# Gated recurrent attention block: the rest term carried inside the step products, Wi's product in whole float32, and a new loop order

## The reference

```python
def step(carry, xs):                 # over the 128 times
    r = decay * r + kt * vt          # kt = vt = ctx
    retained = qt * r                # qt = layernorm(x)
    inp = retained @ Wi.T + bi
    gate = sigmoid(inp @ Wg.T + bg)
    blended = gate * state + (1.0 - gate) * inp
    state = tanh(blended @ A.T + inp @ Bm.T)
    out = state @ Wo.T + bo
x = x + tanh(g_xattn) * out
h = relu(layernorm(x) @ ternary(W1).T + b1)
x = x + tanh(g_ffn) * (h @ ternary(W2) + b2)
```

## Time and profile before

| | us |
|---|---|
| median of three runs | 314.59 (313.75 to 315.14) |
| span of the profiled execution, first to last instruction | 311.7 |
| what lies around the span (median less span) | 2.9 |
| PE busy in the span | 300.7 (96%) |
| DVE busy | 273.8 (88%) |
| ACT busy | 243.9 (78%) |
| POOL busy | 84.5 (27%) |

### The profile page before, as it was taken

One profiled execution on the slowest core, in us unless ns is written; L12 is line 12 of the kernel. 1 busy time (PEld: TensorE's weight loads), 2 busy tenths in 40 slices (PEclk: granted clock), 3 DMA queues, 4 the chain that ended last, 5 costly groups with the idle time before them and its releaser, 6 DMA issues. The chain is left out here.

```text
span 311.7 us, 9499 instructions
## 1 busy us (share of the span) xinstructions
PE 300.7 (96%) x3774; PEld 274.0 (88%) x3774; DVE 273.8 (88%) x805; ACT 243.9 (78%) x560; POOL 84.5 (27%) x147
## 2 busy tenths in 40 slices
PE   7989889999999999999999999999999999999995
PEld 5878778899999999999999999999999999997884
DVE  5987999999999999999999989998999998978763
ACT  4698668978878787978878787879878787857693
POOL 3533053131413214132314123132314121141230
PEclk9999999999999999999999999999999999999999
DMA  7933116142423434443414334444414224170321
GB/s 261 403 109 75 68 36 137 37 67 82 99 42 128 64 137 69 137 67 108 87 49 119 53 136 69 137 70 134 69 53 118 39 70 67 71 103 36 67 36 67
DMA packets 19564, 29.45 MB, mean 94 GB/s; under 512 B 1856, under 2 KB 10304, under 8 KB 19392
## 3 DMA queue, kind: packets, MB, share of 16 engines
q0 software_dynamic: 8720, 8.39, 19.0%
q1 hardware_dynamic: 10368, 19.93, 18.5%
q10 hardware_dynamic: 432, 0.53, 0.5%
HBM read 16.26 MB, written 4.19 MB: 66 GB/s over the span
## 5 line engine op out<-in xcount | busy, mean ns | idle before, releaser
L480 ACT ACTIVATE state<-pre_ps,sc 128x64 f32<-128x64 f32 x128 | 40.1, 313 | 40.0 <-PE pre_ps L1080 39.1
L470 ACT ACTIVATE hid<-hid_ps,b_s 128x256 f32<-128x256 f32 x120 | 50.3, 472 | 11.0 <-PE hid_ps L1119 8.6
L1119 PE MATMUL hid_ps<-xt_lo,w_q 128*128 128x256 f16 x240 | 55.5, 272 | 0.0
L1131 PE MATMUL y_ps<-w_q,h_lo 128*128 128x256 bf16 x240 | 55.5, 272 | 0.0
L1119 PE MATMUL hid_ps<-xt_hi,w_q 128*128 128x256 f16 x240 | 55.5, 272 | 0.0
L1131 PE MATMUL y_ps<-w_q,h_hi 128*128 128x256 bf16 x240 | 55.5, 272 | 0.0
L749 DVE TENSOR_TENSOR h_lo<-hid,h_hi 128x512 f16<-128x512 f32 x60 | 41.3, 688 | 5.7 <-ACT h_hi L476 5.2
L1074 PE MATMUL pre_ps<-m_hi,a_hi 128*128 128x32 f16 x508 | 42.6, 178 | 2.6 <-DVE m_hi L698 2.2
L1074 PEld LDWEIGHTS pre_ps<-m_hi,a_hi 128*128 128x128 f16 x508 | 33.5, 96 | 9.1 <-DVE m_hi L698 4.9
L1074 PE MATMUL pre_ps<-m_hi,a_lo 128*128 128x32 f16 x508 | 41.4, 176 | 0.0
L476 ACT CAST h_hi<-hid 128x512 f16<-128x512 f32 x60 | 37.1, 618 | 1.9
(11 more groups left out here) (183 smaller groups left out, 894.7 us busy)
## 6 DMA issues: line engine op xcount, KB each, us to landing
x_norm<-x_rows_in SPq DMA_DIRECT2D x16, 256.0 KB, 2.8
cx<-ctx_in SPq DMA_DIRECT2D x16, 256.0 KB, 3.4
x_res<-x_in SPq DMA_DIRECT2D x16, 256.0 KB, 3.7
x_res<-bo_g POOLq DMA_DIRECT2D x16, 256.0 KB, 4.8
x<-b_g POOLq DMA_DIRECT2D x15, 256.0 KB, 3.9
y_out<-y SPq DMA_DIRECT2D x15, 256.0 KB, 2.0
w_raw<-w_in SPq DMA_DIRECT2D x2, 512.0 KB, 7.1
w_raw<-w_in SPq DMA_DIRECT2D x1, 1024.0 KB, 9.4
```

The costliest lines, as they stand in the source:

```text
L470: last = nc.scalar.activation(hid[:, p % 2, u, :], hid_ps[p % 2][:, u * N:(u + 1) * N], ACT.Relu, bias=b1_s[:, 2 * p + u:2 * p + u + 1], s ...
L480: nc.scalar.activation(state[:, q[1] % 2, :, step_cols(j)], pre_ps[q[1] % 2][:, :].rearrange("p (k n) -> p k n", k=K)[:, :, step_cols(j)], ...
L1119: last = nc.tensor.matmul(hid_ps[p % 2][:, u * N:(u + 1) * N], w1_q[:, k, cut], v[:, par, k, :], start=n == 0, stop=n == len(terms) - 1)
L1131: last = nc.tensor.matmul(y_ps[:, t * D:(t + 1) * D], h[:, f, t * P:(t + 1) * P], w2_q[:, f, :], start=f == 0 and t == 0 and h is h_hi, st ...
```

## The change

1. **The rest term.** With `u = inp`, g s + (1 - g) u = g (s - u) + u. So A (g s + (1 - g) u) + Bm u = A g (s - u) + (A + Bm) u. From chunk 1 on, `gated_state` computes `mix` = unit s - inp (one instruction more), then `m_hi`, `m_all` = mix x gate and `m_lo`. `rest_all`, `rest_high`, `rest_low` and `from_rest` remain for chunk 0 alone.
2. **A + Bm.** `c_sum` is loaded as Bm a second time (SP, behind the weights) and A is added by a transfer with accumulation from POOL's queue; ACT makes `c_hi` and DVE `c_lo` in chunk 0's body. `from_inp` uses them from chunk 1 on.
3. **A carried scale.** s - u has no bound of 1, so fp16 needs a scale. POOL carries a bound of r from chunk to chunk (`bound_of`, three small instructions, fed by a sum that ACT's `square` now writes out), PE sums it over partitions (`bound_product`, one matmul with a column), ACT adds the bias bound (`bound_out`), DVE takes its power of two and the reciprocal (`unit_of`, two instructions on one column), POOL scales the bias and tanh's factor (`scales_of`, two). `inp_out`, `gate_out` and `tanh_step` take these scales as columns.
4. **Wi's product** goes as 4 matmuls in float32 with `wsq[WI]` and `ret`; `wi_hi`, `wi_lo`, `ret_hi`, `ret_lo` are gone.
5. **A new order** of all queues in the bodies (below), `gate_product` in two parts, `finish` in slot 0 and not 2, the last y products in slot 7.

The new order of a steady body, slot by slot (what stands behind each step):

| slot | DVE | PE | ACT |
|---|---|---|---|
| 0 | finish, state_low | hidden 0, 1 | hidden 0, its high part, bound_out |
| 1 | retain, norm_stats | output 0, 1, hidden 2 | hidden 1, carry, square |
| 2 | hidden_low 0, residual | inp block 0, y 0 | high 1, hidden 2 |
| 3 | unit_of, x1_stats, norm_mean, x1_mean | inp block 1, hidden 3, y 1 | high 2, inp_out 0, 1, inp_high |
| 4 | hidden_low 1, x1_apply | gate_high, y 2 | hidden 3, high 3 |
| 5 | inp_low, hidden_low 2 | y 3, x1_t, gate_low, y 4 | normed_high, gate_out |
| 6 | scan | from_inp 0, 1, y 5 | norm_apply |
| 7 | hidden_low 3, normed_low | bound_product, y 6, 7, and normed_t of the next body | state_high of the next body |

The core of the diff:

```diff
+            def bound_of(q):
+
+                n = number(q)
+                pool.wait_ge(squared, upto(q))
...
+                nc.gpsimd.tensor_tensor(old_part[:, :], bounds[:, 0:1].to_broadcast([P, 2]), by_old[:, :], ALU.mult)
+                nc.gpsimd.tensor_tensor(new_part[:, :], sq_sum[:, q[1] % 2:q[1] % 2 + 1].to_broadcast([P, 2]), by_new[:, :],
+                                        ALU.mult).then_inc(parted, 1)
+                pool.wait_ge(parted, upto(q))
+                nc.gpsimd.tensor_tensor(bounds[:, 0:2], old_part[:, :], new_part[:, :], ALU.add).then_inc(bounded, 1)
...
+            bound_of(NEXT_CHUNK)
+            pool.wait_ge(wsq_in_s[WA], 16)
+            pool.wait_ge(bm_again, 16)
+            pool.dma_start(c_sum[:, :, :], wsq[WA][:, :, :], accum_op=ALU.add).then_inc(c_added, 16)
...
+                if project:
+                    scales_of(project)
+                if attend:
+                    rstd2_of(attend)
+                    add_b2(attend)
                 if norm:
+                    bound_of(norm)
                     rstd1_of(norm)
...
+                    shift1_of(norm)
                 if chain and peeled != NC - 1:
...
+                    add_bo(chain)
...
                 norm_apply(NEXT_CHUNK)
+                bound_out(NEXT_CHUNK)
                 tanh_step(CHUNK, 1)
                 half_sum(1)
+                carry(NEXT_CHUNK)
                 tanh_step(CHUNK, 2)
-                ret_high(NEXT_CHUNK)
-                scaled_high(wo_hi, WO, S_WO)
+                square(THIRD)
+                act.wait_ge(c_added, 16)
+                nc.scalar.mul(c_hi[:, :, :], c_sum[:, :, :], S_A).then_inc(act_prep, 1)
                 tanh_step(CHUNK, 3)
+                inp_out(NEXT_CHUNK, 0)
+                inp_out(NEXT_CHUNK, 1)
+                inp_high(NEXT_CHUNK)
+                tanh_step(CHUNK, 4)
                 half_sum(2)
-                inp_out(NEXT_CHUNK)
-                tanh_step(CHUNK, 4)
-                half_sum(3).then_inc(act_prep, 1)
                 tanh_step(CHUNK, 5)
                 gate_out(NEXT_CHUNK)
+                half_sum(3).then_inc(act_prep, 1)
                 tanh_step(CHUNK, 6)
-                rest_high(NEXT_CHUNK)
+                scaled_high(wo_hi, WO, S_WO)
                 tanh_step(CHUNK, 7)
...
+                if exists(plus(q, -1)):
+                    if j == 0:
+                        dve.wait_ge(inp_set, upto(q, K))
+                    nc.vector.scalar_tensor_tensor(out=mix[:, :, :], in0=before, scalar=unit[:, par:par + 1],
+                                                   in1=inp[:, par, :, step_cols(j)], op0=ALU.mult,
+                                                   op1=ALU.subtract).then_inc(mix_set, 1)
+                    if j == 0:
+                        dve.wait_ge(gate_set, upto(q))
+                    dve.wait_ge(mix_set, upto(plus(q, -1), T, j + 1))
+                    nc.vector.tensor_tensor(m_hi[:, :, :], mix[:, :, :], now, ALU.mult).then_inc(m_hi_set, 1)
+                    nc.vector.tensor_tensor(m_all[:, :, :], mix[:, :, :], now, ALU.mult).then_inc(m_all_set, 1)
+                    dve.wait_ge(m_all_set, fed(q, j))
+                    nc.vector.tensor_tensor(m_lo[:, :, :], m_all[:, :, :], m_hi[:, :, :], ALU.subtract).then_inc(m_lo_set, 1)
+                    return
...
+            def unit_of(q):
+
+                par = q[1] % 2
+                dve.wait_ge(bound_set, number(q))
+                nc.vector.tensor_scalar(inv_unit[:, par:par + 1].bitcast(i32), inp_bound[:, :].bitcast(i32), 0x7F800000, None,
+                                        ALU.bitwise_and).then_inc(inv_unit_set, 1)
+                dve.wait_ge(inv_unit_set, number(q))
+                nc.vector.reciprocal(unit[:, par:par + 1], inv_unit[:, par:par + 1]).then_inc(unit_set, 1)
...
                 gated_state(CHUNK, 7)
+                scaled_low("wo", wo_hi, wo_lo, WO, S_WO)
...
                 threshold()
...
                 dve.wait_ge(pool_prep, pdone["sc"])
                 gates_of_columns()
...
+                if chain:
+                    gated_state(chain, 7)
+                if ffn:
+                    hidden_low(ffn, 3)
+                if attend:
+                    normed_low(attend)
...
+                if ffn and peeled == NC - 1:
+                    finish(ffn)
+                if peeled == NC - 1:
+                    end_residual(0)
...
+            def inp_product(q, m):
+                if m == 0:
+                    pe.wait_ge(ret_set, upto(q))
+                    if exists(plus(q, -1)):
+                        pe.wait_ge(bound_set, number(q))
+                for k in range(K):
+                    last = nc.tensor.matmul(inp_ps[:, m * N:(m + 1) * N], wsq[WI][:, k, m * P:(m + 1) * P], ret[:, k, :],
+                                            start=k == 0, stop=k == K - 1)
+                last.then_inc(inp_sum, 1)
+
+            def gate_high(q):
                 pe.wait_ge(inp_hi_set, upto(q))
                 high_terms(ret_ps, wg_hi, wg_lo, inp_hi)
...
+                high, low = (c_hi, c_lo) if exists(plus(q, -1)) else (bm_hi, bm_lo)
...
                 step(CHUNK, 1)
+                bound_product(NEXT_CHUNK)
                 normed_t(NEXT_CHUNK)
                 keep_warm(4)
                 step(CHUNK, 2)
+                inp_product(NEXT_CHUNK, 0)
+                inp_product(NEXT_CHUNK, 1)
+                step(CHUNK, 3)
...
-                step(CHUNK, 7)
-                from_rest(NEXT_CHUNK)
```

More of the change, by code:

```diff
@@ L334, in _ @@
             pool.wait_ge(xh1_set, 1)
[L335 removed]
             whole_low("wg", wg_hi, wg_lo, WG)
+            growth()
+            bound_of(CHUNK)
             pool.wait_ge(dve_prep, done["inv"])
@@ L381, in _ @@
+                if chain and peeled != NC - 1:
+                    add_bo(chain)
+            run(body, first)
             for t in range(TILES):
@@ new lines, in inp_high, with bound_out @@
+            def inp_high(q):
+                act.wait_ge(inp_set, upto(q, K))
+                nc.scalar.copy(inp_hi[:, :, :], inp[:, q[1] % 2, :, :]).then_inc(inp_hi_set, 1)
+            def bound_out(q):
+                act.wait_ge(bound_sum, number(q))
+                if q is NEXT_CHUNK:
+                    nc.scalar.copy(bias_bound[:, :], inp_ps[:, 1:2]).then_inc(act_prep, 1)
+                    act.wait_ge(act_prep, adone["bias_bound"])
+                nc.scalar.activation(inp_bound[:, :], inp_ps[:, 0:1], ACT.Identity,
+                                     bias=bias_bound[:, :]).then_inc(bound_set, 1)
@@ new lines, in body @@
+                if chain:
+                    tanh_step(chain, 0)
+                if ffn:
+                    hidden(ffn, 0)
+                    hidden_high(ffn, 0)
+                if project:
+                    bound_out(project)
+                if peeled == 1:
+                    side_sign(0)
+                if chain:
+                    tanh_step(chain, 1)
+                if ffn:
+                    hidden(ffn, 1)
+                if norm:
+                    carry(project)
+                    square(norm)
@@ new lines, in body @@
+                peeled = c[1]
+                if chain:
+                    gated_state(chain, 0)
+                if exists(plus(c, -3)):
+                    finish(plus(c, -3))
+                if attend:
+                    state_low(attend)
+                if peeled == 2:
+                    ternary(4)
+                if chain:
+                    gated_state(chain, 1)
+                if project:
+                    retain(project)
+                if norm:
+                    norm_stats(norm)
@@ new lines, in body @@
+                if peeled == 1:
+                    ternary(0)
+                if peeled == 2:
+                    ternary(5)
+                if chain:
+                    gated_state(chain, 2)
+                if ffn:
+                    hidden_low(ffn, 0)
+                if attend:
+                    residual(attend)
+                if chain:
+                    gated_state(chain, 3)
+                if project:
+                    unit_of(project)
+                if attend:
+                    x1_stats(attend)
@@ new lines, in body @@
+                if project:
+                    inp_low(project)
+                if ffn:
+                    hidden_low(ffn, 2)
+                if peeled == 1:
+                    ternary(1)
+                if peeled == 2:
+                    ternary(7)
+                if peeled == NC - 1:
+                    end_state_low(0)
+                if chain:
+                    gated_state(chain, 6)
+                if norm:
+                    scan(norm)
+                if chain:
+                    gated_state(chain, 7)
@@ L1283, in _ @@
+                if chain:
+                    step(chain, 7)
+                if norm:
+                    bound_product(norm)
+                if ffn:
```

(2 more changed lines are left out.)

528 lines of the change are left out of this document (285 added, 243 removed).

## The result

The changed kernel takes 323.43 us (323.17 to 323.77) against 314.71 for the kernel before, run beside it on the same chip: ratio 1.030, 95% interval [1.0275, 1.0318]. It is slower by 8.7 us and lies above the range of 308.5 to 319.5. The span of the profiled execution grew from 311.7 to 321.4. That is 9.7 and not 8.7, because the profiled execution of the kernel before was one of its shorter ones. So the 2.9 us that were taken to lie around its span are too many: in the changed kernel's profiled execution it is 323.17 - 321.4 = 1.8. The forecast difference of -1.0 does not depend on it.

The account below looks back on a forecast made before the run. PE was taken to bound the steady body, with DVE 1.3 us behind. Start +1.5, steady -3.7 and -0.6, tail +1.8 gave -1.0: span 310.7, time 313.6 us against 314.59, range 308.5 to 319.5.

Parts of the forecast that it names:

- PE's own work: Steady body on PE: 17.39 - 3.0 + 1.85 = 16.25 us, with ends 15.5 and 18.0.
- The wait at `gate_high`: PE, steady body: waits for inp_high, 2.1 us of path against 1.6 of cover, so about 0.5 us a body.
- The sum of the two queues: Steady body: PE and DVE queues of 16.75 to 17.0 wait for each other, 17.05 us, ends 16.5 and 17.7.
- DVE: Steady body on DVE: 16.08 - 1.8 + 2.7 = 17.0 us, ends 16.4 and 17.2, longer than PE by a little.
- The step's path, ACT and POOL: Steady body: step path from 1.33 to about 1.6 us, ACT below 14, POOL gains some 1.2 of idle time.
- the third rival: POOL's five new instructions cost DVE up to 1.0 us a body: 18.0 a body, 325 us; chance 0.05.
- The start: Everything up to chunk 3, with chunk 0 and bodies 1 and 2: +1.5 us in all.
- The walk through chunk 0: Tanh by tanh from 19.5 us to chunk 1's first tanh at 35.6 against 33.98: +1.6, ends +0.5 and +3.5.
- Bodies 1 and 2: Body 1 loses the rest term, -0.6 us; body 2 is DVE's, 19.2 against 18.83, +0.4.
- The tail: Last body and after: later residual behind hidden_low 3, y 6 and y 7, +1.8 us, ends +0.7 and +2.3.
- The last body's steps: Body 15: its seven steps are set by the step's path, some +0.5 us.
- The slower one: Each body, a tanh comes 0.5 late without DVE slack: 17.5 us a body, 319.2 us; chance 0.23.

Follow-up runs that it names:

- the single piece: Kernel before with only Wi's product in float32, its eight records in one piece: 317.74 us, ratio 1.0117.
- The pair of edits: Changed kernel with y 2 ahead of gate_high (320.19 us), with a constant for the column in mix (319.97 us), and with both (315.2 us).
- the kernel with y 2 ahead: Changed kernel with product y 2 moved ahead of gate_high in slot 4 of PE's queue: 320.19 us, ratio 1.019.
- the run with a wide one on POOL: Changed kernel with y 2 ahead of gate_high and hidden_low 3 computed on POOL in place of DVE: 329.2 us, ratio 1.049.

## Why the prediction failed, step by step

Between the forecast of -1.0 and the +9.7 of the spans lie 10.7 us: 8.3 in the twelve bodies from chunk 3 on, 1.9 in the start and 0.5 in the tail.

**PE's own work: forecast 16.25, measured 16.75.** This is the first step that failed; its terms were mis-sized. Wi's product was put at 8 x 0.22 = 1.76; it takes 1.90, because each of its two pieces stands behind a step, and there the first record has 0.30 to the next start where the others have 0.22: +0.14. By the four passes that the Trainium skill states ("FP8 and Floating Point Precision", TensorE Precision Notes) I had worked out 2.0, with an fp32r record's 0.126 for a pass; with the 0.11 from start to start of the 16-bit matmuls of the same width, sixteen passes are an estimate of 1.74, and the single piece's 1.73 agrees. `bound_product` was put at 0.1 and takes 0.22 (160.17 to 160.39): +0.12. Splitting `gate_product` makes 1.62 of 1.50 (154.00 to 155.06 and 156.60 to 157.16): +0.12; the change's list has the split, my sum didn't. And the three terms gave back 1.44 and not 1.51: +0.07. These are 0.45 of the 0.50. The rest no run isolates; the timelines show 0.08 at `from_inp`, which stood behind a y product whose last matmul has 0.03 to the next start (153.17 to 153.20 in the kernel before), and now, behind a step, leaves the y products their 0.11.

**The wait at `gate_high`: forecast 0.5, measured 0.72.** The mechanism was right: its place, its releaser, the cover of 1.6. The path was taken from the earlier trace rows as 1.83 and 0.3; there `inp_out` had a constant as scale. With a column the pair takes 1.37 and not 1.18. The Trainium skill ("ScalarE: Activation LUTs", What ACT_TABLE_LOAD costs) gives about 93 ns for each column operand of an ACTIVATE; 787 - 693 = 94 agrees. I had priced the column on DVE, from the earlier trace rows, and not on ACT.

**The sum of the two queues.** I took two queues of 16.75 to 17.0 and 17.05 for the pair, with DVE's a little longer. The pair of edits shows that in the changed kernel the waits add on PE's path: 16.75 + 0.72 + 0.2 = 17.7. PE stands at `gate_high` for ACT, and again at steps 1 and 3 for DVE's `m_lo`. The forecast's 16.25 + 0.5, and 0.25 for small waits at the steps, was a sum of the same form: the form held, and the first two terms were too small. PE's own work had been given an upper end of 18.0, which the body's upper end of 17.7 and the range left out.

**DVE.** `mix` was forecast at 0.25 to 0.27 long and 0.30 in the queue; it is 0.277 and 0.31 to 0.32. Its work was forecast at 17.0 with an upper end of 17.2; with its waits the queue is 17.43 once PE leaves it the lead, 17.2 of it work. In the changed kernel itself it is not the bound. Casting it as "the longer queue by a little" was wrong there, and right for the kernel with y 2 ahead.

**The step's path, ACT and POOL.** ACT at 13.76 fell below 14, as forecast. In the changed kernel's trace ACT stood on `c_added` for 0.22. POOL's busy time rose by 2.0 a body and not 1.2, but its small instructions left DVE's lengths as they were, so the third rival didn't happen in this change; the run with a wide one on POOL shows that its mechanism exists.

**The start: forecast +1.5, measured +3.4.** The walk through chunk 0 held nearly to the end: tanhs at 21.6, 23.0, 25.8, 27.9, 30.1, 32.25, 33.65 against 21.6, 23.2, 25.8, 27.7, 29.9, 32.0, 33.3 forecast, and chunk 1 at 36.27 against 35.6. Bodies 1 and 2 failed: +0.4 and +0.7 against -0.6 and +0.4. Without the scale they are 16.89 and 18.92, that is -0.4 and +0.1, so part of the gain of the removed rest term was there, and the scale took it. In both runs body 1 has a mean granted clock of 0.90, with 3.4 us of it at 1.2 GHz, where the kernel before had 1.00; in the changed kernel PE had been busy for only 3.94 us of 6.00 and then 0.73 of 1.75 before it fell. What that costs body 1 no run isolates.

**The tail: forecast +1.8, measured +2.3.** The distance from last `m_hi` to first residual is 3.31, forecast 3.4, and the order undone gives it back. The last body's steps were put at +0.5; from its first tanh to the last `m_hi` it is 12.55 against 11.59, +1.0: `mix` puts 0.31 on each step's path, and the 1.0 is a good third of eight times 0.31; no run isolates this part.

**The rivals.** The slower one gave 17.5 a body and 319.2, by a late tanh without slack on DVE. Its direction was right; its mechanism was not the one found, since the largest loss is PE standing for `inp_hi`, which I had in the forecast itself. A late tanh is there: tanh 4 stands behind `inp_high` and DVE waits 0.25 for it. But PE has `gate_high` and y 2 to do meanwhile and does not wait for that step. What was missing was a rival in which one cause, the carried scale, brings the steady bodies and the start to their bad ends together.

## What to carry to other kernels

When an edit takes work off the bound engine and puts a handover to another engine in its place, the new period can be the engine's own work plus each handover's uncovered rest, summed, as here, and not the longer of two queues; place enough ready work behind each handover, and check that it is ready. A scale that is read per step costs in every step: fold it into an operand that is made once per chunk, on the engine that stands idle there (here 0.48 a body, 17.43 to 16.95). Before a wide operation goes to GpSimd to relieve VectorE, look at which short VectorE operation it will meet.
